# The causal mask of the second attention: from selects on the exponentials to matmuls into the score banks

## What is computed

```
q, k, v = split of x @ Wq, x @ Wkv                 # 16 heads of 8 channels
dots = einsum('bhid,bhjd->bhij', q * 8**-0.5, k)   # 256 x 256 for each head
dots = where(tril, dots, -50000)                   # query i sees keys j <= i
attn = softmax(dots)
out = einsum('bhij,bhjd->bihd', attn, v) @ Wo
```

## Time and profile before

| | value |
|---|---|
| median of three runs | 2515.79 us |
| the profiled execution's own time | 2517.02 us |
| its span, first to last instruction | 2515.3 us |
| TensorE busy | 2225.9 us (88%) |
| VectorE, ScalarE, GpSimd busy | 66%, 66%, 31% |
| mean granted TensorE clock | 0.941 |
| second attention, first to last select | 1026.0 to 1675.5 us |

### The profile page before, as it was taken

How to read it: one execution, slowest core, us unless ns; L and a number is a source line. 1 busy time by engine, 2 the same in 40 slices (tenths; PEclk the granted TensorE clock), 3 DMA queues, 4 the chain that set the end, 5 groups by cost and what they waited for, 6 DMA issues and landing times.

```text
span 2515.3 us, 49710 instructions
## 1 busy us (share of the span) xinstructions
PE 2225.9 (88%) x15074; PEld 1087.4 (43%) x15074; DVE 1649.1 (66%) x3569; ACT 1653.4 (66%) x2585; POOL 780.6 (31%) x1625
## 2 busy tenths in 40 slices
PE   5688888888668996999999999976799999999998
PEld 5544444444433333344444444445344444444443
DVE  5355555554678777566666666657666676676766
ACT  2366666667368784244444444446799999999997
POOL 2333333331223335244444444434222212222222
PEclk9999999999579996699999999985899999999999
DMA  4000000000100000000000000011000000000000
GB/s 130 5 1 0 0 0 0 0 0 1 42 9 0 0 0 34 1 1 0 0 0 0 0 0 0 0 68 33 1 5 10 4 8 4 4 8 4 4 9 9
DMA packets 22284, 24.92 MB, mean 10 GB/s; under 512 B 3024, under 2 KB 20304, under 8 KB 21200
## 3 DMA queue, kind: packets, MB, share of 16 engines
q1 hardware_dynamic: 19456, 23.17, 2.8%
q10 hardware_dynamic: 2768, 1.00, 0.2%
HBM read 19.91 MB, written 4.26 MB: 10 GB/s over the span
## 4 chain that ended last, share of the span: by engine, by line
PE 49%; DVE 4%; issue 3%; ACT 2%; DVEq 2%; POOLq 0%; POOL 0%; ACTq 0%
PE OP L1440 13%; PE SP L1420 13%; PE OP L1275 6%; PE M L1234 4%; PE M L1190 2%; PE M L1204 2%; DVE mx L852 2%; PE SP L1255 2%; PE M L1230 2%; PE M L1430 2%; PE M L1225 1%; ACT shared L512 1%; PE SP L1150 1%; PE OP L1304 1%; PE SP L1140 1%
## 5 line engine op out<-in xcount | busy, mean ns | idle before, releaser
L531 ACT ACTIVATE pt<-SP 128x1024 f32<-128x1024 f32 (+1 forms) x512 | 459.7, 921 | 366.3 <-PE SP L1255 366.2
L1033 DVE TENSOR_TENSOR pt<-vs,pt 128x512 f16<-128x512 f32 x640 | 497.4, 783 | 269.2 <-ACT vs L596 266.4
L594 ACT ACTIVATE pt<-SP,b 128x512 f16<-128x512 f32 x640 | 447.0, 698 | 117.7 <-PE SP L1420 116.7
L596 ACT ACTIVATE vs<-SP,b 128x512 f32<-128x512 f32 x640 | 449.4, 702 | 0.0
L1275 PE MATMUL OP<-pt,vs 128*32 128x256 f32 (+1 forms) x4096 | 434.9, 362 | 15.3 <-ACT pt L531 13.8
L401 POOL TENSOR_TENSOR st<-st,ksT 128x512 f32<-128x512 f32 x160 | 213.4, 1334 | 737.0 <-DVE ksT L1050 736.9
L1420 PE MATMUL SP<-hT,shared 128*128 (+1 forms) x1536 | 355.1, 381 | 0.0
L1440 PE MATMUL OP<-pt,shared 128*128 128x512 f16 x1536 | 353.5, 380 | 0.0
L852 DVE TENSOR_REDUCE mx<-M 128x2 f32<-128x512 f32 (+1 forms) x384 | 257.1, 691 | 118.0 <-PE M L1234 114.8
L1275 PEld LDWEIGHTS OP<-pt,vs 128*32 128x32 f32 x4096 | 177.1, 110 | 182.6 <-issue 53.1
L1420 PEld LDWEIGHTS SP<-hT,shared 128*128 128x128 f16 x1536 | 149.4, 98 | 177.7 <-issue 3.0
(11 more groups left out here) (167 smaller groups left out, 2919.5 us busy)
## 6 DMA issues: line engine op xcount, KB each, us to landing
rows<-g_dram SPq DMA_DIRECT2D x4, 2048.0 KB, 7.5
x_sb<-in_x SPq DMA_DIRECT2D x8, 512.0 KB, 8.9
pt<-in_w SPq DMA_DIRECT2D x4, 1024.0 KB, 7.5
out<-x_sb SPq DMA_DIRECT2D x16, 256.0 KB, 2.3
pt<-in_w SPq DMA_DIRECT2D x4, 256.0 KB, 5.5
pt<-in_wmod SPq DMA_DIRECT2D x2, 384.0 KB, 3.6
wqkv<-in_wqkv ACTq DMA_DIRECT2D x2, 192.0 KB, 6.0
gateB<-gate_dram SPq DMA_DIRECT2D x1, 256.0 KB, 3.0
```

Source lines behind the costliest of these rows:

```text
L531: act.activation(pt[:, u % 4, :, 0:W], SP[u % 2][:, :, 0:W], ACT.Exp, scale=SCALE).then_inc(s["exp"], 1)
L594: act.activation(hid[:, e % 2, f, 0, :], bank[k % 4], ACT.Relu, bias=b1[l][:, k:k + 1], scale=1.0 / WSCALE)
L596: act.activation(relu[:, k % 4, :], bank[k % 4], ACT.Relu, bias=b1[l][:, k:k + 1], scale=1.0 / WSCALE).then_inc(s["relu"], 1)
L1033: dve.tensor_tensor(hid[:, e % 2, f, 1, :], relu[:, k % 4, :], hid[:, e % 2, f, 0, :], ALU.subtract).then_inc(s["lo"], 1)
```

## The change

The two selects and the tiny operation are gone from GpSimd's stream, and with them the drain ahead of select 0, the semaphore `sel` and the tile `spare`. In the second attention each score unit now opens with two matmuls, one a head: weights `maskQ`, moving operand `identb` read twice (256 columns), written to the two diagonal blocks with `start=True`. The four score matmuls then add with `start=False`. `values` waits for `exp`. The first attention keeps its instructions.

```diff
-                def select(b, u):
-                    pool.wait_ge(s["exp"], CH * b + u + 1)
-                    pool.tensor_tensor(spare[:, u:u + 1], ones[:], ones[:], ALU.mult)
-                    for i in range(2):
-                        diag = pt[:, u % 4, i, :].rearrange("p (k q) -> p k q", k=2)[:, :, 0:P]
-                        last = pool.affine_select(out=diag, in_=diag, compare_op=ALU.is_ge, fill=0.0, base=0,
-                                                  pattern=[[0, 2], [1, P]], channel_multiplier=-1)
-                    last.then_inc(s["sel"], 1)
-
                 def one(b, par, first=False, ahead=3):
-                    if l:
-                        pool.drain()
-                        select(b, 0)
                     if ahead >= 1:
                         place_v(b + 1, 1 - par, first)
-                    if l:
-                        for u in range(1, CH):
-                            select(b, u)
...
                     j = u // 2
+                    if l:
+                        for i in range(2):
+                            diag = SP[u % 2][:, i, 0:TT * T].rearrange("p (k q) -> p k q", k=TT)[:, :, 0:P]
+                            pe.matmul(diag, maskQ[:], identb[:].unsqueeze(1).to_broadcast([P, TT, P]),
+                                      start=True, stop=False, skip_group_check=True)
                     for k in range(TT):
                         q0 = P if (l and k) else 0
                         for i in range(2):
                             r0 = 32 * (2 * (u % 2) + i)
                             last = pe.matmul(SP[u % 2][:, i, k * T:k * T + T - q0],
                                              ksT[r0:r0 + 32, par, j, k * P:(k + 1) * P], qsT[r0:r0 + 32, par, j, q0:T],
-                                             start=True, stop=True, tile_position=(r0, 0))
+                                             start=(l == 0), stop=True, skip_group_check=True, tile_position=(r0, 0))
...
-                    pe.wait_ge(s["sel" if l else "exp"], CH * b + u + 1)
+                    pe.wait_ge(s["exp"], CH * b + u + 1)
```

More of the change, by code:

```diff
@@ L98, in program @@
         ones = sb("ones", [P, 1])
-        spare = sb("spare", [P, CH])
         maskQ = sb("maskQ", [P, P], BF16)
@@ L185, in program @@
         norm_s = [sems("norm", n, "z zT h hT x xin gelu " + ("rexp wload0 wload1 whi wlo" if n % 2 else "gmm gsum")) for n in range(4)]
-        att_s = [sems("att", l, "h proj sel qkv stack sT sE mfill mred mrow score exp pv o oT an aT aE wo wr x kE guess rn vs")
+        att_s = [sems("att", l, "h proj qkv stack sT sE mfill mred mrow score exp pv o oT an aT aE wo wr x kE guess rn vs")
                  for l in range(2)]
```

## The result

The changed kernel takes 2571.12 us (median; 2569.18 to 2580.86), the kernel before 2515.72 (2515.42 to 2516.63): a ratio of 1.0227, with a 95% interval of 1.0202 to 1.0253. The profiled execution took 2571.09 us, 54 more than the one of before. The forecast was 2590 in a range of 2565 to 2618: slower, as forecast, by three quarters of the amount.

The account below looks back on a forecast made before the run. TensorE's own stream was taken as the bound. 2.30 us a batch x 31 = 71.3, plus 1 for the last batch and 1.7 for the first: 74 on 2517.0 gives 2591, median 2590 us; range 2565 to 2618.

Parts of the forecast that it names:

- The bound: Second attention: TensorE's own stream sets the pace, nobody waits for GpSimd, so the selects' going gives nothing in steady batches.
- rival of the selects on the path: Selects close the batch at unit 7; their going gives back 0.97 us a batch, total 2485 us; chance 0.02.
- columns only: Gaps vanish in waits; a mask unit costs 0.213 us, 1.28 a batch, total 2557 us; chance 0.11.
- Units 0 and 1: Masks split their eight score matmuls: 0.90 us more a batch, hidden in 0.92 of slack before the sixteen transposes.
- the cover is gone: The 0.90 us of units 0 and 1 shows in full: 2618 us; chance 0.12 for half or more.
- Unit 2: Its mask group stands behind full transposes: +0.32 us a batch.
- Unit 3: Its score matmuls lose the shadow of the `prep_max` group ahead: 0.91 in place of 0.31 us, +0.60.
- Units 4 to 6: Their mask groups stand behind a values group: +0.32 us each, 0.96 a batch.
- Unit 7: Cut apart from `prep_max` 11: 0.91 in place of 0.49 us, +0.42 a batch.
- the edge: First and last batches: +1.7 us for masks at the 0.50 clock in the first, net +1 in the last.
- the main case's own range: 2577 to 2603 us, from 0.05 us more or less a mask group; the main forecast had chance 0.73.
- The rule on modes: Changing tiling mode drains TensorE, about 0.11 us each; every unit pays a drain into the mask and one out.

Follow-up runs that it names:

- the doubled masks: Changed kernel with every mask matmul issued twice: 2624.12 us (one run), steady batch 24.12 us.
- Filling the waits: Kernel before, selects kept, `prep_max` masks in 32-row tiles, plus thrown-away full-array matmuls in TensorE's two recurring waits: 2563.8 us, ratio 1.0186.
- the pairs: Kernel before, selects kept, `prep_max` groups taken two at a time, both masks ahead of both sets of row-group matmuls: 2567.03 us, ratio 1.0203.

## Why the prediction was right, and where its sizes were off

**The bound.** Right: with the selects gone the steady batch didn't move (20.38), and with masks and selects together it is the changed kernel's 22.52. The rival of the selects on the path is dead, and so is "columns only": 0.32 a group, not 0.21.

**The terms.** Measured between the same groups of both traces, with these two rows of the kernel before beside the earlier trace rows:

```profile
1317.86 0.91 PE L1190 MATMUL M<-wqkv,ha 128*128 128x384 f32 x2 [0.40 <-ACT shared L512]
...
1326.10 0.84 PE L1275 MATMUL OP<-pt,vs 128*32 128x256 f32 x8
```

Units 0 and 1, from the projection's second tile to the transposes, take 2.55 us before (1317.86 to 1320.41) and after (1381.10 to 1383.66), so the 0.90 is hidden whole, with 0.1 to spare by the doubled masks; the rival "the cover is gone" did not happen. Unit 2, +0.22 (forecast 0.32). Unit 3, +0.60 (0.60). Units 4 to 6, +0.97 (0.96). Unit 7, +0.43 (0.42). Between the tail's second transposes and the next values, 2.58 before and 2.51 after, -0.07 (none in the sum). Unrounded that makes 2.14 against 2.30.

**The step that was mis-sized in the batch** is unit 2: "behind full transposes, +0.32". Sixteen transposes take 1.00 us up to row-group scores, but only 0.90 up to a mask, full array like themselves (1383.66 to 1384.56). So the change of mode was paid once either way, at the mask's far side, and I had counted it twice. The same 0.09 at unit 0 (the projection's tile takes 0.75 to a mask, 0.84 to the scores) is the 0.1 us of cover left over. Over 29 steady batches unit 2's 0.10 and the 0.07 are the 4.7 us by which they came out cheaper.

**The step that failed** is the edge: "in the first batch the clock is 0.50 in places", priced at +1.7. I took the clock of before as given and charged the masks for it. In fact the first batch got 7.3 us shorter, because the clock came up early: the forecast had 2.3 + 1.7 = 4.0 us more for it, so 11.3 us lie between forecast and trace here. The rest of the 20 us between 2591 and 2571 (profiled executions): 4.7 in the 29 steady batches; 1.7 behind the last transposes, where batch 30's masks and the last batch were forecast at 2.3 + 1 = 3.3 and took 1.6; and 2.3 gained ahead of the first batch. With the slow stretch back, as in the kernel with no masks in batches 0 and 1, the total is 2577.68, just inside the main case's own range.

**The rule on modes** held. The Trainium skill, TensorEngine Tiling (Array Packing), section Key Properties, has the change of mode drain TensorE; the same mask without a change of mode, in 32-row tiles, cost 0.58 us a batch instead of 2.14. What one change costs is measured here: 0.09 to 0.11 us.

**What stays open.** What makes the granted clock fall. In the steady part it stayed at 1.00 in the ten kernels whose batch at full clock was 20.38 us or longer, and fell again and again in the four whose batch was shorter (20.08, 19.24, 18.89, 18.89). Filling the waits did not help. Neither the lack of full-array masks (the pairs have them) nor idle time is the cause alone. Open too is why the clock comes up early in most runs of the changed kernel, by their mean clocks, but only in few of the ten with masks in the first two batches alone. No version that applies the mask was found to beat the kernel before.

## What to carry to other kernels

On an engine that sets the pace, cost an added matmul by distances between starts, with a gap for each change between full array and row or column groups, and add what it cuts apart; put it beside work of its own mode, or cut it into tiles of its neighbours' mode. Work taken from an engine that nobody waits for is worth nothing: here 233 us of GpSimd time bought 3 at most. And look at the granted clock before trusting a shorter stream: a batch that is 7% shorter at full clock made the kernel about 2% slower or worse.

## What the runs showed of the hardware that was not expected

- More TensorE work made a stretch shorter: with the masks the first batch took 22.00 us in place of 29.30, as the granted clock was 1.00 instead of 0.50. With masks in the first two batches only, the runs spread from 2510.74 to 2521.73 us.
- A busy TensorE does not by itself hold the clock. With fillers it was busy 487 of 500 us at a mean of 0.82; the kernel before is busy 470 of 500 at 1.00. The Trainium skill, TensorE: Matmul & The Clock Gate, section Why this matters for your kernels, advises to keep TensorE continuously busy so as to reach the high clock, and to leave no idle gaps so as not to drop from it; these two stretches show that the profile's busy share is not the measure of that.
- Eight 32-row matmuls of 64 columns, in two row groups, take 0.13 us together, less than two full ones of 256 columns with the same mask (0.21 without their gap).
